# A four-layer network on one core: the second layer's block with its router's weights loaded early and another planned order

## The chip, the cores and the metric
The kernel runs on one core of one Trainium2 chip. The metric is the device time of one execution in microseconds.

## What is computed
A network of four layers on 2048 tokens of 128 features. Each layer adds an attention-like branch and an expert branch to x, both computed from the normalised x. The change touches the second layer alone:

```python
def _L1_attn_ref(x, Wq, Wk, Wv, Wf, g_norm_w, Wo):
    q = _swish((x @ Wq).reshape(b, t, H, K))
    k = _swish((x @ Wk).reshape(b, t, H, K))
    v = (x @ Wv).reshape(b, t, H, V)
    f = jax.nn.log_sigmoid((x @ Wf).reshape(b, t, H, M)) / GATE_LOGIT_NORMALIZER
    s = 1.0 - jnp.exp(f)
    o = _gsa_recurrence(q, k, v, s, f, scale=K ** (-0.5))
    o = o * jax.lax.rsqrt(jnp.mean(o * o, axis=-1, keepdims=True) + NORM_EPS) * g_norm_w
    return o.reshape(b, t, H * V) @ Wo

def _L1_ffn_ref(tokens, gate_w, W1, b1, W2, b2):
    probs = jax.nn.softmax(x @ gate_w.T, axis=-1)
    top2_w, top2_idx = jax.lax.top_k(probs, 2)
    counts = jnp.bincount(top2_idx.reshape(-1), length=E)
    keep = (counts <= cap).astype(x.dtype)
    comb = jnp.zeros((T, E), dtype=x.dtype).at[jnp.arange(T)[:, None], top2_idx].add(top2_w)
    comb = comb * keep[None, :]
    h = jax.nn.relu(jnp.einsum('th,ehf->tef', x, W1) + b1[None, :, :])
    y = jnp.einsum('teh,ehf->tef', h, W2) + b2[None, :, :]
    out = jnp.einsum('te,tef->tf', comb, y)
```

The recurrence keeps, per head, a state that is decayed by gates at every token; the kernel computes it in chunks of 64 tokens.

## The kernel before
Features lie on the 128 partitions, tokens along them. The tokens are two halves of 1024, and all is f32. The function `layer_1_branches` holds the whole second layer's block: the attention branch for both halves and the expert branch (eight experts, four quarters of 512 tokens, 32 steps j) run interleaved on TensorE, ScalarE and VectorE.

The attention branch, for each half: `projections` multiply the tokens with the weights `wt` (keys, values, gates by token; L1536), four pairs of products, each pair copied from PSUM by ScalarE (L1737). `log_of_sigmoid` forms the gates on ScalarE (absolute value L1744, exponential L1748, logarithm L1752), VectorE ends them in `gates` (L1879). `sums_of_gates` (L1554, L1556) and `gates_at_ends` (L1568, 16 products with 4 columns) sum them over tokens; `queries_or_keys` are products with `wq` through `product` (L108), `added` (L1586) makes what every chunk adds to the state, `states` (L1905) chains the 14 chunks on VectorE in 28 operations, which end with the scaling at L1911, and `states_turned` (L1597) turns them by 64 small products. Then come eight tiles of 128 tokens for each half: keys by queries (L1611, L1616), the mask on VectorE (L1922), logits (L1626), a softmax over VectorE and ScalarE (L1935 to L1954), transposes (L1635, L1638), their copy by ScalarE (L1831), slots by slots (L1649), a mask (L1962), outputs (L1659, L1664). At the end the mean of squares, the norm and the product with `wo`.

The expert branch: the router's product (`routing.logits`, L1007) and its choices on VectorE, an exponential on ScalarE (L1030), the counts (L1018), the turn to rows (L1024) and a store of the routing weights `comb` to memory (L995). From there SyncE loads a row of `comb` spread over all partitions for each step (`l_cs`, L1494) and a small piece for the bias product (`l_comb`, L1484). Step j: the first product (L108, tile `l_w1s`), relu on ScalarE (L1864), the weighing on VectorE (L1990), the second product summed in PSUM (L1716). Each quarter's sum starts with the bias product (L1713) and is added to x by VectorE (L1997). Three buffers hold the hidden values and the spread rows.

The order on each engine is written by a plan: every operation is a generator step that yields a planned time, and `in_order` sorts an engine's steps by these times (`PLAN_HALF` by half, `PLAN_TILE` by tile, `PLAN_EXPERT` by step). The same times set which of three PSUM slots a result takes, and so what it must wait for:

```python
def in_order(*programs):
    ahead = [[next(p, None), p] for p in programs]
    while any(time is not None for time, p in ahead):
        first = min((n for n, (time, p) in enumerate(ahead) if time is not None), key=lambda n: ahead[n][0])
        ahead[first][0] = next(ahead[first][1], None)
```

Only the order of the times matters, not their values. Semaphores carry all dependences, so a step waits if its inputs are late. Blocks of different layers are separated by a barrier of all engines.

Of the kernel before, what the change touches and what calls it, by code (L numbers as in the profile page):

```python
# [12 lines left out]
D = 128  # L13
# [33 lines left out]
class Core:  # L47
# [27 lines left out]
    def sem(self, name):  # L75
        self.taken.append(self.nc.alloc_semaphore(name))
        return self.taken[-1]
# [1154 lines left out]
def layer_0_output(core, cols, x1):  # L1232
# [4 lines left out]
    with ExitStack() as ctx:  # L1237
# [41 lines left out]
    "raw": ((-1081.249, -1077.137, -1042.271, -1024.881), (-1011.753, -941.228, -773.834, -752.792)),  # L1279
    "copy_raw": ((-1075.619, -1037.111, -970.597, -922.579), (-711.412, -622.755, -601.399, -519.594)),  # L1280
    "q": ((-475.959,), (451.442,)),
    "q_silu": ((-172.152,), (588.372,)),
    "k": ((-326.269,), (583.701,)),
    "kt_silu": ((-126.114,), (703.013,)),
    "abs": ((-878.111,), (-516.284,)),
    "exp": ((-725.621,), (-409.285,)),
    "ln": ((-674.441,), (-217.181,)),
    "f": ((-925.510,), (-654.044,)),
    "expf": ((-588.789,), (43.256,)),
    "s": ((-887.741,), (-81.622,)),  # L1290
    "D": ((-714.095, -640.152, -317.000, -294.344), (-249.299, 133.889, 490.244, 533.240)),
    "decays": ((-556.237, -351.939, -94.621, -14.229), (-66.260, 511.555, 656.344, 668.213)),
    "eg": ((-381.908, -343.173, -118.829, 45.012), (55.472, 548.470, 686.294, 691.310)),
    "weights": ((-692.871, -671.130, -211.073, -102.260), (-74.956, 121.898, 490.122, 561.874)),
    "ends": ((-644.216,), (-219.247,)),
    "decay_ends": ((-272.821,), (125.503,)),
    "add": ((-129.287, -108.606), (665.011, 676.767)),
    "copy_add": ((421.957, 453.205), (764.074, 794.772)),
    "states": ((-57.796, -18.779, 171.653, 263.587), (652.682, 702.699, 710.536, 745.507)),
    "scale": ((334.169,), (750.775,)),  # L1300
    "Skt": ((625.370,), (1350.808,)),
    "copy_Skt": ((709.734,), (1295.597,)),
    "square": ((1352.872,), (1411.883,)),
    "mean": ((1421.698,), (1491.541,)),
    "log": ((2544.424,), (3617.117,)),
    "rstd": ((3341.839,), (4064.410,)),
    "scaled": ((3612.555,), (4066.440,)),
    "out": ((4071.457,), (5267.780,)),
    "join": ((4089.228,), (4246.270,)),
    "k_silu": ((-180.112,), (171.365,)),  # L1310
}
PLAN_TILE = {
    "A": (704.440, 1365.757),
    "mask_A": (651.820, 1450.125),
    "L": (710.156, 1370.819),
    "lg": (658.341, 1456.286),
    "soft": (805.839, 1338.538),
    "norm": (659.343, 1459.812),
    "T": (717.401, 1378.542),
    "copy_T": (809.914, 1344.911),  # L1320
    "B": (718.082, 1380.008),
    "mask_B": (665.065, 1464.168),
    "O": (723.357, 1384.516),
    "copy_O": (814.259, 1350.264),
}
PLAN_EXPERT = {
    "hidden": (-986.666, -848.766, -723.734, -624.912, -407.809, -325.502, -258.983, -133.205, -80.466, 302.035, 474.836, 531.890, 625.094, 661.711,
        711.318, 718.337, 738.819, 766.229, 822.014, 1225.173, 1360.244, 1373.418, 1381.800, 1402.399, 1418.613, 1428.896, 2604.976, 3173.687,
        3563.369, 4059.409, 4177.355, 4298.075),
    "relu": (-732.131, -624.941, -552.867, -304.909, -180.719, -129.717, -79.314, 141.992, 193.548, 521.253, 624.829, 697.552, 707.962, 735.468,  # L1330
        806.695, 819.352, 840.576, 857.238, 1214.835, 1291.321, 1318.674, 1345.054, 1356.302, 1379.255, 1393.381, 2575.189, 3350.433, 3501.179,
        3565.950, 4065.778, 4246.291, 4292.431),
    "weigh": (-752.536, -727.210, -694.226, -656.618, -471.742, -408.385, -249.266, -96.387, 40.067, 61.793, 125.045, 550.246, 562.989, 646.471,
        677.977, 687.350, 695.614, 790.153, 1362.310, 1409.461, 1449.578, 1467.566, 2536.958, 3282.350, 3320.613, 3469.474, 3567.542, 3583.767,
        4070.138, 4114.201, 4123.695, 4124.013),
    "add": (-595.909, -377.501, -333.886, -226.051, -190.628, -166.810, 3.203, 37.949, 580.705, 598.643, 629.913, 705.892, 712.623, 716.751, 752.963,
        755.712, 824.914, 1364.972, 1366.185, 1372.704, 1388.344, 1416.763, 1446.606, 1448.758, 3170.214, 3404.566, 3591.788, 3989.248, 4250.325,
        4302.464, 5146.025, 5160.432),
    "cs": (-919.034, -843.901, -830.537, -394.140, -306.056, -305.801, -204.452, -109.561, 349.895, 351.828, 373.491, 454.101, 607.007, 687.599,
        690.334, 750.696, 750.930, 1361.245, 1368.714, 1420.148, 1496.241, 2548.207, 2548.946, 3158.556, 3355.408, 3360.017, 3427.646, 3595.730,  # L1340
        4140.388, 4174.676, 4182.187, 4307.648),
    "b2": (-638.253, 509.912, 810.290, 2570.119),
    "join": (20.309, 715.071, 3462.675, 4126.088),
# [1824 lines left out]
```

## Time and profile before

| | us |
|---|---|
| three runs | 1866.88, 1859.01, 1863.92 |
| median | 1863.92 |
| the profiled execution | 1868.61 |
| its span | 1866.9 |
| mean granted TensorE clock | 0.949 |
| TensorE busy over the span | 1695.0 (91%) |
| VectorE busy | 1310.5 (70%) |
| ScalarE busy | 1229.2 (66%) |

The span is what the profiler's instructions cover; the execution's own time is 1.7 us longer. Names in the profile have no number (`l_raw` is `l1_raw0` or `l1_raw1`); PE is TensorE, PEld its weight loads, DVE VectorE, ACT ScalarE, SP SyncE, whose queue issues the loads. A product of 512 columns in f32 shows as two records, so that "x2" stands for one of them.

### The profile page before, as it was taken

The page shows a single profiled execution, that of the slowest core. Times are in us where ns is not written, and L with a number is a line of the kernel's source. Part 1 is how long each engine was busy: PE and PEld are TensorE (multiplying, and loading weights), DVE is VectorE, ACT ScalarE, POOL GpSimd, SP SyncE. Part 2 cuts the span into 40 slices and gives each one's busy share as a digit, 9 for nine tenths or more (in the row PEclk, how much of TensorE's full clock was granted, in tenths as well). Part 3 has the DMA queues.
Part 4 walks back from the last instruction along what each step waited for, and adds up shares of the span by engine and source line. Part 5 has one row for each costly group of instructions (what it writes and reads, how often), then busy time and mean ns, then how long its engine had stood idle before and what let it go on. Part 6 is the DMA issues. An engine that isn't in the chain of part 4 may idle for free. (4 is left out here: it accounts for less than half of the span.)

```text
span 1866.9 us, 19526 instructions
## 1 busy us (share of the span) xinstructions
PE 1695.0 (91%) x6936; PEld 700.4 (38%) x6944; DVE 1310.5 (70%) x1793; ACT 1229.2 (66%) x1541; POOL 109.2 (6%) x159
## 2 busy tenths in 40 slices
PE   4599999999999999996899599997898989997998
PEld 2133333333333333322443356563243333333665
DVE  4677777777777777741333237773999999996897
ACT  2488888888888888883132287334786767772663
POOL 1000111111111111011000100000000000000000
PEclk8799999999999999998799699998899999999999
DMA  3400000000001000000131121111344444541000
GB/s 102 131 6 12 23 12 23 12 24 12 24 12 24 12 7 12 1 1 2 59 113 56 33 54 47 42 29 28 110 139 158 146 158 141 171 162 34 6 1 23
DMA packets 48136, 100.76 MB, mean 54 GB/s; under 512 B 7719, under 2 KB 21126, under 8 KB 46740
## 3 DMA queue, kind: packets, MB, share of 16 engines
q1 hardware_dynamic: 48042, 99.54, 17.2%
q8 instruction: 55, 0.90, 0.2%
q14 instruction: 39, 0.32, 0.1%
HBM read 91.55 MB, written 7.87 MB: 53 GB/s over the span
## 5 line engine op out<-in xcount | busy, mean ns | idle before, releaser
L727 DVE TENSOR_REDUCE best<-quad 128x2 f32<-128x1024 f32 x256 | 309.6, 1221 | 130.5 <-PE quad L517 128.0
L641 ACT ACTIVATE weights<-quad 128x1024 f32<-128x1024 f32 x256 | 255.4, 1027 | 28.9 <-PE quad L542 28.6
L108 PE MATMUL quad<-xn,l_w1s 128*128 128x512 f32 x288 | 151.1, 632 | 9.8 <-DMA l_w2s<-in_F_w 7.6
L2400 ACT ACTIVATE l_hid<-quad,l_w1s 128x512 f32<-128x512 f32 x112 | 75.2, 686 | 99.5 <-PE quad L108 98.9
L559 PE MATMUL quad<-weights,values 128*32 128x512 f32 x1024 | 136.4, 605 | 0.4 <-ACT weights L641 0.4
L2262 PE MATMUL quad<-l_st,ident 128*128 128x512 f32 x256 | 121.3, 602 | 5.8 <-DVE l_st L2466 5.7
L108 PE MATMUL quad<-q,wf 128*128 128x512 f32 x256 | 121.5, 606 | 0.7 <-DVE mk L698 0.3
L2308 PE MATMUL quad<-l_hid,l_w2s 128*128 128x512 f32 x224 | 105.7, 601 | 15.5 <-DVE l_hid L2497 15.5
L108 PE MATMUL quad<-hid,wf 128*128 128x512 f32 x256 | 116.6, 599 | 0.0
L585 ACT ACTIVATE hid<-quad,col 128x512 f32<-128x512 f32 x128 | 84.7, 686 | 21.7 <-PE quad L108 21.5
L517 PE MATMUL quad<-ks,qs 48*128 48x512 bf16 x512 | 89.5, 385 | 7.0 <-DVE best L727 6.4
L542 PE MATMUL quad<-qs,ks 49*128 49x512 bf16 x512 | 91.5, 384 | 2.2 <-ACT weights L641 2.2
L1213 ACT ACTIVATE e_hid<-quad,e_w1s 128x1024 f32<-128x1024 f32 x32 | 35.6, 1113 | 83.7 <-PE quad L108 83.7
L108 PE MATMUL quad<-sq_all,mean_w 128*128 128x512 f32 x176 | 89.6, 621 | 0.2 <-POOL sq_all L753 0.2
L108 PE MATMUL quad<-cur,wa 128*128 128x512 f32 x168 | 87.1, 627 | 0.0
L1229 DVE TENSOR_TENSOR e_hid<-e_hid,e_cs 128x1024 f32<-128x1024 f32 x32 | 38.5, 1222 | 67.5 <-ACT e_hid L1213 48.0
L108 PEld LDWEIGHTS quad<-xn,l_w1s 128*128 128x128 f32 x288 | 53.0, 196 | 86.3 <-issue 54.1
L2449 DVE TENSOR_TENSOR l_st<-l_u,l_bs 128x1024 f32<-128x1024 f32 x64 | 76.0, 1213 | 3.2 <-PE quad L2262 3.2
L753 POOL TENSOR_TENSOR sq_all<-cen_all 128x512 f32<-128x512 f32 x64 | 65.2, 1039 | 217.2 <-DVE cen_all L672 217.2
L542 PEld LDWEIGHTS quad<-qs,ks 49*128 49x128 bf16 x512 | 22.2, 93 | 146.8 <-issue 60.4
L2466 DVE TENSOR_TENSOR l_st<-l_st,l_c_rows 128x1024 f32<-128x1024 f32 x64 | 75.9, 1214 | 0.0
L2262 PEld LDWEIGHTS quad<-l_st,ident 128*128 128x128 f32 x256 | 49.2, 194 | 70.3 <-issue 59.4
(379 smaller groups left out, 3064.4 us busy)
## 6 DMA issues: line engine op xcount, KB each, us to landing
l_bs<-xd_dram SPq DMA_DIRECT2D x32, 512.0 KB, 4.8
l_c_rows<-xd_dram SPq DMA_DIRECT2D x32, 512.0 KB, 4.6
l_cs<-comb SPq DMA_DIRECT2D x28, 512.0 KB, 4.8
e_cs<-comb SPq DMA_DIRECT2D x8, 1024.0 KB, 5.2
l_cs<-comb SPq DMA_DIRECT2D x32, 256.0 KB, 3.3
wf<-in_L_f SPq DMA_DIRECT2D x16, 256.0 KB, 2.6
l_w1s<-in_F_w SPq DMA_DIRECT2D x28, 129.0 KB, 2.1
l_w2s<-in_F_w SPq DMA_DIRECT2D x28, 128.0 KB, 2.3
```

The lines of the kernel that those rows point to most:

```text
L108: last = nc.tensor.matmul(out[:, c:c + BANK], lhsT, rhs[:, c:c + BANK], start=(n == 0), stop=(n == len(pairs) - 1))
L517: last = nc.tensor.matmul(to[:, par * BANK:(par + 1) * BANK], qs[n % BUFS][rows, slot, qt * P:(qt + 1) * P], ks[n % BUFS][rows, slot, c * ...
L542: last = nc.tensor.matmul(to[:, par * BANK:(par + 1) * BANK], ks[n % BUFS][rows, slot, kt * P:(kt + 1) * P], qs[n % BUFS][rows, slot, c * ...
L559: last = nc.tensor.matmul(out[32 * j:32 * j + 32, :], values[:, kt, GH * g + j, :], weights[p % BUFS][:, j % 2, j // 2, :], start=(kt == 0 ...
L585: return nc.scalar.activation(*args, ACT.Gelu_apprx_tanh, **kwargs)
L641: nc.scalar.activation(weights[p % BUFS][:, slot, :, :].rearrange("p a t -> p (a t)"), doubles.of("weigh", m, i), ACT.Exp, scale=scale).th ...
L727: nc.vector.tensor_reduce(heads[:, :, slot, qt, c], doubles.of("search", m, i).rearrange("p (a t) -> p a t", a=2), AX.X, ALU.max).then_inc ...
L2262: last = nc.tensor.matmul(y[d][:, c:c + BANK], core.ident[:, :], st[n % RING][:, c:c + BANK], start=False, stop=(s == NS - 1), skip_group_ ...
L2308: last = nc.tensor.matmul(total[c], w2s[p][:, f, :], hid[j % HIDS][:, f, :], start=False, stop=False, skip_group_check=True)
L2400: nc.scalar.activation(hid[j % HIDS][:, f, :], ring.of("hidden", j, f), ACT.Gelu, bias=w1s[p][:, F + f:F + f + 1]).then_inc(hidden_read, 1)
L2449: nc.vector.tensor_tensor(st[n % RING][:, :], u[h][d][:, :], bs[k % 2][:, :], ALU.mult).then_inc(dbx_ready, 1)
L2466: nc.vector.tensor_tensor(st[n % RING][:, :], st[n % RING][:, :], cs_rows[k % 2][:, :], ALU.mult).then_inc(times_c, 1)
```

## The change
Three edits. The router's weights are loaded second instead of eighth. The load of the query and key weights `wq` counts on a semaphore of its own, on which each of the four products with `wq` waits; the start of TensorE's program waits for `wt` alone. And all planned times of the block are new, of which two lines of 62 stand here:

```diff
 PLAN_HALF = {
-    "raw": ((-1081.249, -1077.137, -1042.271, -1024.881), (-1011.753, -941.228, -773.834, -752.792)),
+    "raw": ((-1580.895, -1575.614, -415.628, -352.666), (-1568.371, -350.926, -286.483, -159.875)),
...
-    landed, wo_landed, built = sem("landed"), sem("wo_landed"), sem("built")
+    landed, wq_landed, wo_landed, built = sem("landed"), sem("wq_landed"), sem("wo_landed"), sem("built")
...
                 sp.dma_start(wt[:, :], a["A1_tok"]).then_inc(landed, 16)
-                sp.dma_start(wq[:, :], a["A1_qk"]).then_inc(landed, 16)
+                routing.load(sp)
+                sp.dma_start(wq[:, :], a["A1_qk"]).then_inc(wq_landed, 16)
                 sp.dma_start(wo[:, :], a["A1_wo"]).then_inc(wo_landed, 16)
                 for h in range(GH4):
                     sp.dma_start(gain[GK * h:GK * h + GK, :], a["A1_gain"]).then_inc(wo_landed, 16)
-                routing.load(sp)
...
                 def queries_or_keys(h, name, ready):
                     u = "qk".index(name)
                     yield pre(name, h)
+                    pe.wait_ge(wq_landed, 16)
                     ring_free(pe, name, h, 0)
...
-                pe.wait_ge(landed, 32)
+                pe.wait_ge(landed, 16)
```

From the edit at `wq_landed` on, lines of the changed kernel are one higher. What the new times move is shown at three places. The first is ScalarE's start of the block: copies of the tokens' products (L1737, now L1738), the absolute value, the routing's exponential. Before:

```order
L1737 ACTIVATE l1_raw0<-quad0 128x1024 x2
L1737 ACTIVATE l1_raw0<-quad1 128x1024
L1737 ACTIVATE l1_raw0<-quad0 128x1024
L1744 ACTIVATE l1_se0<-l1_raw0 128x2048
L1730 ACT_TABLE_LOAD
L1030 ACTIVATE l1_route_exps<-l1_route_exps 128x128
L1864 ACTIVATE l1_hid0<-quad1,l1_w1s 128x512
```

And now:

```order
L1738 ACTIVATE l1_raw0<-quad0 128x1024 x2
L1738 ACTIVATE l1_raw1<-quad1 128x1024
L1738 ACTIVATE l1_raw0<-quad0 128x1024
L1731 ACT_TABLE_LOAD
L1030 ACTIVATE l1_route_exps<-l1_route_exps 128x128
L1738 ACTIVATE l1_raw0<-quad0 128x1024
L1745 ACTIVATE l1_se0<-l1_raw0 128x2048
L1865 ACTIVATE l1_hid0<-quad1,l1_w1s 128x512
```

The routing's exponential has moved ahead of the absolute value and of the first half's last copy; the third copy is of the second half. The second place is VectorE behind the routing: weighings of hidden values, the gates (L1879, now L1880). Before:

```order
L1098 COPY l1_route_turned_comb<-quad1 128x128
L1879 SCALAR_TENSOR_TENSOR l1_raw0<-l1_raw0,l1_se0 128x8x256
L1883 TENSOR_SCALAR l1_add0<-l1_add0 128x2048
L1990 TENSOR_TENSOR l1_hid0<-l1_hid0,l1_cs0 128x512
L1990 TENSOR_TENSOR l1_hid1<-l1_hid1,l1_cs1 128x512
```

And now:

```order
L1098 COPY l1_route_turned_comb<-quad1 128x128
L1991 TENSOR_TENSOR l1_hid0<-l1_hid0,l1_cs0 128x512
L1991 TENSOR_TENSOR l1_hid1<-l1_hid1,l1_cs1 128x512
L1880 SCALAR_TENSOR_TENSOR l1_raw0<-l1_raw0,l1_se0 128x8x256
L1991 TENSOR_TENSOR l1_hid2<-l1_hid2,l1_cs2 128x512
```

Two weighings, each with its spread row from memory, now stand ahead of the first half's gates. The third place is TensorE at the end of the first half's last two tiles (transposes L1638, slots L1649, outputs L1659 and L1664; each one higher now). Before:

```order
L1638 MATMUL quad0<-ident,l1_lg2 128x128 x2
L1649 MATMUL quad0<-l1_turned2 128x128 x4
L1659 MATMUL quad0<-l1_Am2,l1_raw0 32x128 x4
L1664 MATMUL quad0<-l1_turned2,l1_add0 32x64 x8
L1635 MATMUL quad0<-ident,l1_se0 128x128 x2
L1638 MATMUL quad0<-ident,l1_lg3 128x128 x2
L1649 MATMUL quad0<-l1_turned3 128x128 x4
L108 MATMUL quad1<-xn,l1_w1s 128x512
L1659 MATMUL quad0<-l1_Am3,l1_raw0 32x128 x4
```

And now:

```order
L1639 MATMUL quad0<-ident,l1_lg2 128x128 x2
L1717 MATMUL quad1<-l1_hid0,l1_w2s 128x512
L1650 MATMUL quad0<-l1_turned2 128x128 x4
L1598 MATMUL quad1<-l1_zeros,l1_add1 32x64 x4
L1598 MATMUL quad1<-ident,l1_add1 32x64 x60
L1660 MATMUL quad0<-l1_Am2,l1_raw0 32x128 x4
L1665 MATMUL quad0<-l1_turned2,l1_add0 32x64 x8
L1636 MATMUL quad0<-ident,l1_se0 128x128 x2
L1639 MATMUL quad0<-ident,l1_lg3 128x128 x2
L1717 MATMUL quad1<-l1_hid1,l1_w2s 128x512
L1650 MATMUL quad0<-l1_turned3 128x128 x4
L108 MATMUL quad1<-xn,l1_w1s 128x512
```

Two expert sums and the turning of the second half's states, which came after the tiles, stand between them now. In the second half's tiles, in turn, five tiles in a row have no expert product between them; before there was one in most.

## Rows read from the trace of the kernel before

**Rows 1.** Windows: length, busy us of PE, PEld, DVE, ACT, POOL; PEclk, DMA, GB/s
```profile
1059.00:1275.00 216.00, 202.53 (x1819) 122.81 (x1819) 130.89 (x303) 109.11 (x154) 4.92 (x31) 0.92 0.19 48
1099.00:1104.00 5.00, 5.00 (x7) 1.76 (x7) 1.29 (x2) 3.47 (x5) 0.00 (x0) 0.50 0.58 90
1145.00:1190.00 45.00, 44.25 (x661) 29.89 (x660) 37.79 (x92) 21.32 (x35) 0.00 (x0) 1.00 0.14 39
1194.00:1200.00 6.00, 5.31 (x42) 2.61 (x38) 5.02 (x18) 1.15 (x3) 0.00 (x0) 0.50 0.00 0
```

**Rows 2.** Timeline, block's start: start us, us, engine, line, operation, count [idle before <-releaser]
```profile
1059.34 0.34 SPq L1464 DMA_DIRECT2D l_wt<-in_A_tok  x1
...
1059.72 0.43 SPq L1465 DMA_DIRECT2D l_wq<-in_A_qk  x1
...
1062.54 0.42 SPq L987 DMA_DIRECT2D l_route_w<-in_F_router  x1
...
1064.29 5.90 PE L1007 MATMUL quad<-l_route_w,xn 128*128 128x8 f32 x27 [9.70 <-DMA l_route_w<-in_F_router]
```

**Rows 3.** DMA issues of 1059 to 1064 us: KB each, us to landing
```profile
l_wt<-in_A_tok SPq DMA_DIRECT2D x1, 256.0 KB, 2.7
```

**Rows 4.** DMA issues of 1290 to 1300 us, the third layer's start
```profile
l_route_w<-in_F_router SPq DMA_DIRECT2D x1, 7.0 KB, 4.3
```

**Rows 5.** Timeline, the routing's exponential and what waits for it
```profile
1080.93 1.91 ACT L1744 ACTIVATE l_se<-l_raw 128x2048 f32<-128x2048 f32 x1
...
1085.93 0.39 PE L1018 MATMUL quad<-l_route_load,mean_w 128*128 128x8 f32 x2 [1.80 <-DVE l_route_load L1084]
...
1092.07 0.67 PE L1554 MATMUL quad<-l_raw,l_rel 128*128 128x256 f32 x2 [0.38 <-ACT l_raw L1737]
```

**Rows 6.** Timeline, the store of the routing weights, spread rows and gates
```profile
1087.75 0.60 SPq L995 DMA_DIRECT2D comb<-l_route_turned_comb  x1
1089.88 1.28 SPq L1494 DMA_DIRECT2D l_cs<-comb  x3
...
1089.67 2.29 DVE L1879 SCALAR_TENSOR_TENSOR l_raw<-l_raw,l_se 128x2048 f32<-128x2048 f32 x1 [1.95 <-ACT l_se L1752]
```

**Rows 7.** Tile l_cs, all 32 loads of the block
```profile
DMA to landing us min/median/max: 3.0/3.3/6.0
```

**Rows 8.** Timeline of TensorE, end of the first half's tiles; last row from the end
```profile
1192.06 0.71 PE L1649 MATMUL quad<-l_turned 64*128 64x128 f32 x8 [0.69 <-ACT l_turned L1831]
1193.63 0.50 PE L1659 MATMUL quad<-l_Am,l_raw 128*32 128x128 f32 x8 [0.86 <-DVE l_Am L1962]
...
1196.46 1.22 PE L1649 MATMUL quad<-l_turned 64*128 64x128 f32 x8 [0.69 <-ACT l_turned L1831]
1197.61 2.07 PE L108 MATMUL quad<-xn,l_w1s 128*128 128x512 f32 x2
...
1201.81 1.12 PE L108 MATMUL quad<-xn,l_w1s 128*128 128x512 f32 x2
1202.77 1.02 PE L1716 MATMUL quad<-l_hid,l_w2s 128*128 128x512 f32 x2
...
1254.40 1.88 PE L108 MATMUL quad<-sq_all,l_heads 128*128 128x512 f32 x4
```

**Rows 9.** Timeline of TensorE, the second half's tiles
```profile
1209.20 0.71 PE L1611 MATMUL quad<-sq_all,l_kt 64*128 64x128 f32 x8 [0.53 <-ACT l_send L1817]
...
1226.04 0.71 PE L1611 MATMUL quad<-sq_all,l_kt 64*128 64x128 f32 x8
...
1230.50 0.71 PE L1611 MATMUL quad<-sq_all,l_kt 64*128 64x128 f32 x8
...
1235.37 0.72 PE L1611 MATMUL quad<-sq_all,l_kt 64*128 64x128 f32 x8
...
1250.16 0.72 PE L1649 MATMUL quad<-l_turned 64*128 64x128 f32 x8 [0.69 <-ACT l_turned L1831]
```

**Rows 10.** Timeline of VectorE, the scaling that ends a half's states
```profile
1200.02 2.23 DVE L1911 TENSOR_TENSOR l_add<-l_add,l_ends 128x960 f32<-128x960 f32 x2
```

More of the change, by code:

```diff
@@ L1288 @@
[L1288 to L1305, printed above, removed]
@@ new lines @@
+    "weights": ((-50.321, 755.376, 843.753, 848.533), (1514.057, 1525.649, 1680.677, 1729.672)),
+    "ends": ((231.854,), (986.181,)),
+    "decay_ends": ((857.885,), (1098.550,)),
+    "add": ((1574.525, 1584.281), (2102.023, 2112.373)),
+    "copy_add": ((2505.899, 2549.893), (2985.709, 2989.305)),
+    "states": ((1696.355, 1980.000, 2644.887, 2656.230), (2726.647, 2942.474, 2945.464, 2970.313)),
+    "scale": ((2681.014,), (3037.400,)),
+    "Skt": ((2526.495,), (2979.793,)),
+    "copy_Skt": ((3119.875,), (3217.354,)),
@@ L1311 @@
+    "square": ((3238.834,), (13549.288,)),
+    "mean": ((3190.301,), (13506.655,)),
+    "log": ((13419.396,), (13923.299,)),
+    "rstd": ((13889.254,), (13969.301,)),
+    "scaled": ((13416.150,), (13533.290,)),
+    "out": ((13900.092,), (14096.747,)),
+    "join": ((13563.678,), (14097.220,)),
+    "k_silu": ((1190.511,), (1120.572,)),
 }
 PLAN_TILE = {
[L1313 to L1324, printed above, removed]
+    "A": (2923.687, 3134.954),
+    "mask_A": (3031.933, 3219.629),
+    "L": (2929.289, 3140.564),
+    "lg": (3038.201, 3225.124),
+    "soft": (3166.696, 3350.062),
+    "norm": (3042.363, 3226.683),
+    "T": (2936.194, 3147.984),
+    "copy_T": (3170.468, 3352.244),
@@ L1342 @@
[L1342 to L1351 removed]
+    "hidden": (-298.163, -253.668, -140.919, -84.812, 780.855, 919.924, 939.445, 1030.080, 1122.956, 1151.335, 1284.201, 1574.042, 1808.544,
+        2048.518, 2112.350, 2141.572, 2517.344, 2674.724, 2926.783, 2933.188, 2966.161, 2971.943, 2986.234, 3143.206, 3188.193, 3196.659, 3389.005,
+        13236.423, 13483.791, 13510.350, 13563.602, 13886.754),
@@ L1352 @@
+    "b2": (-134.838, 1346.631, 2926.430, 3217.086),
+    "join": (926.530, 2947.016, 3302.077, 13603.221),
+    "comb": (-134.535, 896.909, 1575.183, 2054.189),
+    "route": (-350.152, -317.194, -315.724, -271.617),
+    "logits": (-1699.373,),
+    "count": (-307.419,),
+    "turn": (-294.816,),
+    "choice": (-283.017,),
+    "store": (-314.758,),
+    "stored": (-244.448,),
 }
```

66 lines of the change are left out of this document (30 added, 36 removed).

## The prediction
> **What bounds the kernel now.** I read the engines' busy time over the block first. The second layer's block runs from the issue of its first load at 1059.34 us [rows 2] to about 1275 us. TensorE is busy 202.5 of the 216 us there, VectorE 130.9 and ScalarE 109.1 [rows 1]. So TensorE's work sets the length, and an order of instructions can win only two things: time in which TensorE waits, and time in which it works at the lower of its two clock levels (a granted clock of 0.50, which is 1.2 of 2.4 GHz). The other layers are not touched and are separated from this one by barriers.
>
> Then I read the timeline for TensorE's waits. The largest are: 9.70 us before the first router product, of which 4.95 lie after 1059.34 (the rest belongs to the norm before) [rows 2]; 1.80 us before the product for the counts [rows 5]; three waits of 0.69 to 0.86 us where the first half's last tiles end [rows 8]; 0.53 us for the second half's first tile and 0.69 us at its last [rows 9]. Low clock shows from 1099 to 1104 us, although TensorE was then busy all the time, and from 1194 to 1200 us, behind the first two of the three waits [rows 1, 8].
>
> **The change, part by part.** All terms are against the profiled execution; minus is shorter.
>
> *Start.* TensorE begins when the first tokens' weights and the router's weights have landed. Before, the router's load is the eighth issued, at 1062.54, and the first product starts at 1064.29, 1.75 us after that [rows 2]. Now it is second, issued at 1059.72 where the query and key weights were, and the start no longer waits for those. The tokens' weights land 2.7 us after 1059.34, at 1062.04 [rows 3]. For the router's load standing behind a 256 KB load I have two bounds: those 1.75 us, where it stood behind small loads, and 4.3 us in the third layer, where it is third behind 256 KB [rows 4]. I take 2.7, as the load just ahead of it took: it lands at 1062.4, and **-1.85 us** is won, with bounds -2.2 (the tokens' weights are then the later) and -0.2. The added wait for the query and key weights costs nothing: their first product comes behind the gates' first products, which start at 1092 [rows 5]. On SyncE the router's load passes six others, which are issued one place later; none is wanted before the first expert's weights, which keep their place. Nothing is moved on GpSimd.
>
> *Counts.* ScalarE's exponentials for the routing stood behind the absolute value of 2048 columns, 1.91 us [rows 5]; now they come before it. The product for the counts can start 1.85 + 1.91 earlier, at 1082.17. TensorE has one product of 512 columns fewer ahead of it (0.86 us at full clock: two take 1.88 and one 1.02 with its end [rows 8]) and is free at 1085.93 - 1.80 - 1.85 - 0.86 = 1081.4. The wait shrinks from 1.80 to 0.76: **-1.04**.
>
> *Two new waits right behind.* The bias product of the experts used to come late, behind the gates' products; now it comes behind the counts, the turn (0.35 us for both), three expert products and four of the tokens: 7 x 0.86 + 0.35 later, at 1088.55. The store of the routing weights followed the counts by 1.82 us and the first load from it by 2.13 [rows 6]; so that load is issued at 1086.12, the small one for the bias product at 1086.55, and at 3.0 us to landing, the quickest of the large loads [rows 7], it is there at 1089.55: **+1.0** (bounds 0, if it lands as fast as a store, and +4.0 at the 6.0 us of the slowest load of such rows [rows 7]). Behind it VectorE weighs the first two experts before it forms the gates of the first half (2.29 us, [rows 6]), and the second of these waits for a 256 KB load. Three such loads end 6.0 us after the third's issue, so I put the second's at 4.5 us, 1091.5. The gates are then done at 1091.5 + 0.69 + 2.29 = 1094.5; TensorE wants them at 1093.0 after four more products. That is 1.5 us where 0.38 stood [rows 5]: **+1.1** (0 to +3).
>
> *Entry into the tiles.* The second half's chain of states, 28 small operations that stood among the tiles, now lies nearly whole ahead of the first mask, and the scaling that ends it, 2.23 us on VectorE [rows 10], stands between the first tile's mask and its logits. It is ready about when TensorE's logits are, so it is in the way; TensorE has the next tile's products (about 1.0 us) and an expert product to cover it, and what follows needs the second mask, which is late too, by an estimated 0.4: 2.23 + 0.4 - 1.0 - 0.86 = **+0.8** (0 to +3).
>
> *End of the first half.* There TensorE had nothing of its own to do between a transpose and its copy. Now two expert sums, one expert product and the 64 small products that turn the second half's states stand in exactly these places. The three waits go: 0.69 + 0.86 + 0.69 = **-2.24**. With them should go the low clock behind them: the small products took 1.22 instead of 0.71 us, the expert product 2.07 instead of 1.12, and I estimate 0.2 us for each of the four groups of small products beside them [rows 8]: **-2.3**. The bound is half the 5.3 us busy at that level, -2.65, and 0 if the clock stays low.
>
> *Turned states ready early*, so the second half's first tile need not wait for their copy: **-0.53** [rows 9].
>
> *Tiles without a filler.* In the steady stretch VectorE sets the pace when TensorE has no expert work: 4.46 us for a tile, against 4.87 with a product that takes 0.96 us start to start [rows 8, 9]. A tile without filler thus loses 4.46 - (4.87 - 0.96) = 0.55 us. There were five such tiles, there are eight now, five of them in a row: **+1.65**.
>
> *Tail.* An expert sum fills the 0.69 us before the last tile: **-0.69**. The 21 products behind it find their inputs at the pace of the old ones; the chain of the last norm ends while they run.
>
> Sum: -1.85 - 1.04 + 1.0 + 1.1 + 0.8 - 2.24 - 2.3 - 0.53 + 1.65 - 0.69 = **-4.1 us**. The profiled execution took 1868.6, the median of the three runs is 1863.9; against the median that gives **1859.8 us**. The largest term is the low clock behind the waits, and it is the least sure one. The rows show a fall behind a stretch with waits of at most 0.86 us, and another at 1099 us with TensorE busy throughout [rows 1, 8]. The Trainium skill (TensorE: Matmul & The Clock Gate, "What's actually happening") says that the clock falls after TensorE has been idle for long enough; waits this short would then not have caused the fall, and filling them would not lift it. By that rule the sum would be -1.8.
>
> **The rivals.**
> - *The low clock stays or only moves* (20%). For it: the fall at 1099 shows that full busy time does not protect, and the filler there is partly small products. Against it: from 1145 to 1190 us, where such small products and whole tiles ran, the clock stayed up [rows 1]. Then -2.3 is missing: 1862.1 us.
> - *The early start doesn't happen* (7%). The router's load takes 4.3 us as in the third layer; TensorE starts at 1064.1. Then 1.65 of the 1.85 is missing: 1861.5 us. For it, the only row of a router load close behind a large one; against it, that one had another small load between, and was not waited for alone.
> - *More low clock goes* (20%). The falls in the block's first third (1099 to 1104) follow the tiny products for the gates at the ends, whose surroundings change. If one of them goes too, half of 5 us is won, 2.5, and with the two new waits at their lower bounds 2.1 more: -8.7, or 1855.2 us. If a second of these falls goes, 2.5 more: 1852.7.
> - *Slower: new falls of the clock* (10%). The waits ahead of the gates put idle time right before the tiny products, and five tiles in a row without filler leave TensorE 12% idle. If the clock falls once in each place, each at half of 5.3 us (2.65), and the new waits come out in the middle of their upper halves (+2.5), the result is -4.1 + 5.3 + 2.5 = +3.7: 1867.6 us. It decides as soon as both falls are there. Against it: of the tiles between 1165 and 1190 us three were unfilled, and the clock stayed at 1 [rows 1].
>
> **How the numbers follow.** The forecast itself gets 43%, with 1857 to 1863 as its own range. About 0.5%, 9.3 us, is what a measurement of this kernel can tell from no change. All cases but the best end of the third lie inside it, and the slower rival too; so "same" gets most: faster 0.16 (most of the third rival's lower part, and a spread of the runs of some 4 us either way), slower 0.03, same 0.81. The range 1853.5 to 1866 takes in the first three rivals and half of the slower one.
>
> **What would show it.** In the profile of the changed kernel the first router product should start near 1062.4 us, the counts' near 1082.2, with waits of about 1 us ahead of the bias product and 1.5 us ahead of the gates' products. The first half's last tiles should show no wait over 0.3 us and a granted clock of 1. The block's last sum should end near 1271. A first product at 1064, a low clock between the halves, or a new low stretch in the second half's tiles would each point to its rival. A wait of TensorE over 2 us in the stretch from 1110 to 1160, where I expect none, would show the whole reading wrong.

## The result and the profile after

The changed kernel takes 1861.5 us (median of 20 runs, 1858.1 to 1866.2) against 1867.8 us for the kernel before (20 runs on the same chips, 1858.9 to 1877.5). The ratio is 0.9967, with a 95% interval of 0.9955 to 0.9979: 6.2 us, or 0.33%, faster. The profiled execution took 1860.27 us.

Two executions differ by some microseconds outside the change too: the block's first load is issued at 1059.34 us before and at 1060.86 now, with the same program ahead of it. So I measure the block itself, from the issue of its first load to the end of the last sum into x: 1274.92 - 1059.34 = **215.58 us** before and 1270.23 - 1060.86 = **209.37 us** now, 6.21 less. Over the block TensorE is idle 13.07 us before and 8.97 now; the other 2.11 us are busy time. The work is the same, so busy time differs mainly by the clock at which it is done.

The same windows as [rows 1], of the changed kernel (length, busy us of PE, PEld, DVE, ACT, POOL; PEclk, DMA share, GB/s):

```profile
1061.00:1276.00 215.00, 204.66 (x1829) 124.25 (x1830) 130.52 (x302) 110.35 (x155) 4.79 (x31) 0.94 0.19 48
1100.00:1105.00 5.00, 5.00 (x14) 3.67 (x15) 0.34 (x1) 4.93 (x3) 0.00 (x0) 0.50 0.28 67
1145.00:1190.00 45.00, 44.18 (x589) 27.31 (x588) 41.10 (x114) 22.69 (x33) 0.00 (x0) 1.00 0.17 49
1194.00:1200.00 6.00, 6.00 (x68) 3.91 (x66) 4.65 (x12) 2.61 (x7) 0.00 (x0) 1.00 0.01 3
```

The last row was 5.31 us busy at 0.50 before [rows 1]: the low clock between the halves is gone. The one at 1100 is still there. The block's start and the routing, against [rows 2, 3, 5, 6], from the timeline of the changed kernel, with one row of its DMA issues at the end:

```profile
1060.86 0.34 SPq L1464 DMA_DIRECT2D l_wt<-in_A_tok  x1
...
1061.24 0.42 SPq L987 DMA_DIRECT2D l_route_w<-in_F_router  x1
...
1063.86 6.97 PE L1007 MATMUL quad<-l_route_w,xn 128*128 128x8 f32 x32 [7.75 <-DMA l_route_w<-in_F_router]
...
1084.53 0.39 PE L1018 MATMUL quad<-l_route_load,mean_w 128*128 128x8 f32 x2 [0.72 <-DVE l_route_load L1084]
...
1091.41 1.09 PE L1714 MATMUL quad<-l_comb,l_b2s 8*128 8x512 f32 x2 [0.27 <-issue]
...
1094.13 0.69 DVE L1991 TENSOR_TENSOR l_hid<-l_hid,l_cs 128x512 f32<-128x512 f32 x1 [1.39 <-DMA l_cs<-comb]
1094.74 2.28 DVE L1880 SCALAR_TENSOR_TENSOR l_raw<-l_raw,l_se 128x2048 f32<-128x2048 f32 x1
...
1094.87 1.13 PE L1717 MATMUL quad<-l_hid,l_w2s 128*128 128x512 f32 x2 [0.46 <-DVE l_hid L1991]
...
1097.12 1.03 PE L1569 MATMUL quad<-l_at_ends,l_raw 128*128 128x4 f32 x8 [1.12 <-issue]
```

```profile
l_route_w<-in_F_router SPq DMA_DIRECT2D x1, 4.0 KB, 2.5
```

TensorE's first product starts at 1063.86, 3.00 us after the first issue, where it was 4.95. The counts wait 0.72 instead of 1.80; their product comes 23.67 us after the first issue, where it was 26.59. The second weighing waits for its row of routing weights, and VectorE forms the gates only behind it; TensorE pays 0.46 and 1.12 us for that. These are the new waits that the prediction put at 1.5 us. At the end of the first half [rows 8] TensorE now goes through without a wait:

```profile
1199.13 1.02 PE L1717 MATMUL quad<-l_hid,l_w2s 128*128 128x512 f32 x2
1200.09 0.72 PE L1650 MATMUL quad<-l_turned 64*128 64x128 f32 x8
...
1200.87 1.85 PE L1598 MATMUL quad<-ident,l_add 64*32 64x64 f32 x120
1202.66 0.42 PE L1660 MATMUL quad<-l_Am,l_raw 128*32 128x128 f32 x8
```

**The low clock.** In the first 15 us behind the first issue every version has a granted clock of 0.50 (1.2 of 2.4 GHz). Behind them the kernel before has three stretches at a granted clock of 0.50, the changed one two, and the second is shorter. Windows of exactly these stretches, before and after:

```profile
1098.24:1105.10 6.86, 6.86 (x12) 2.94 (x11) 1.67 (x3) 4.20 (x6) 0.00 (x0) 0.50 0.52 85
1122.18:1128.98 6.80, 6.80 (x28) 3.23 (x31) 1.29 (x2) 3.11 (x5) 0.00 (x0) 0.50 0.11 36
1193.90:1200.70 6.80, 6.11 (x62) 3.02 (x54) 5.76 (x19) 1.56 (x3) 0.00 (x0) 0.50 0.00 0
```

```profile
1099.80:1106.60 6.80, 6.80 (x20) 5.14 (x20) 1.79 (x2) 5.56 (x4) 0.00 (x0) 0.50 0.22 53
1120.30:1123.70 3.40, 3.40 (x9) 2.19 (x9) 0.18 (x1) 3.33 (x6) 0.00 (x0) 0.50 0.33 79
```

So 20.5 us of low clock have become 10.2. In this pair of profiles the norm behind the block gained as well, 3.1 us that the block's length doesn't hold: its eight products on x take 3.67 us instead of 6.75. These are the first product rows behind the block, of the trace before and of the trace after:

```profile
1276.39 6.75 PE L108 MATMUL quad<-x,centre_w 128*128 128x512 f32 x8 [2.73 <-PEq L86]
```

```profile
1271.73 3.67 PE L108 MATMUL quad<-x,centre_w 128*128 128x512 f32 x8 [2.75 <-PEq L86]
```

### The profile page after: what moved, and what is told of

Read it like the earlier page. It is cut to its first block and busy times, and to the rows that moved or that the text cites. A ratio compares the mean times of both kernels' runs of the same rounds, so it can differ in the third digit from the quotient of the medians.

```text
span 1858.5 us, 19528 instructions
## 1 busy us (share of the span) xinstructions
PE 1689.4 (91%) x6936; PEld 700.0 (38%) x6944; DVE 1310.6 (71%) x1793; ACT 1227.5 (66%) x1539; POOL 109.1 (6%) x159
```

## The experiments

Each kernel ran in five rounds beside the kernel before. Since single executions differ by several us, three numbers of each kernel's one profile stand beside the ratio: the block's length as defined above, TensorE's idle time in it, and the time at a clock of 0.50 in it, after the first 15 us (from windows of 2 us, so good to 0.1). A profile is a single execution: a load that lands a microsecond later in it is in these numbers too.

| kernel | ratio to before (95%) | block us | TensorE idle | low clock |
|---|---|---|---|---|
| before | 1 | 215.58 | 13.07 | 20.4 |
| changed | 0.9967 (0.9955 to 0.9979) | 209.37 | 8.97 | 10.3 |
| 1 loads alone | 0.9950 (0.9937 to 0.9964) | 209.39 | 11.50 | 6.8 |
| 2 order alone | 0.9971 (0.9957 to 0.9985) | 212.04 | 11.01 | 13.7 |
| 3 no fillers at the half's end | 0.9999 (0.9987 to 1.0011) | 215.04 | 12.41 | 13.6 |
| 4 gates first | 0.9958 (0.9942 to 0.9974) | 208.19 | 8.03 | 10.2 |
| 5 filled tiles | 0.9960 (0.9946 to 0.9975) | 208.63 | 8.10 | 13.6 |
| 6 small products spread | 0.9977 (0.9968 to 0.9987) | 211.38 | 9.07 | 13.6 |
| 7 = 4 + 5 + 6 | 0.9907 (0.9892 to 0.9922) | 200.82 | 6.97 | 0 |
| 8 loads, fillers on the old order | 1.0006 (0.9997 to 1.0016) | 218.57 | 17.29 | 20.4 |
| 9 = 4 + 6 | 0.9933 (0.9912 to 0.9954) | 203.73 | 8.36 | 0 |
| 10 = 7 without fillers | 0.9944 (0.9924 to 0.9964) | 205.66 | 11.26 | 0 |
| 11 = 7, old loads | 0.9928 (0.9907 to 0.9949) | 204.69 | 10.48 | 3.4 |
| 12 loads, spread, on the old order | 0.9999 (0.9985 to 1.0012) | 215.85 | 13.47 | 17.0 |

Block less idle is TensorE's busy time: 193.9 to 195.4 us where there is no low clock (7, 9, 10), 200.4 with 10.3 us of it (changed), 202.5 with 20.4 (before). The work is the same. So two columns, idle and low clock, explain most of the third, though not all of it: a straight line through the fourteen busy times leaves up to 2.4 us (kernel 3 is busy 202.6 us with 13.6 us of low clock, kernel 8 only 201.3 with 20.4).

### The two parts apart

Loads alone: the plan's tables of the kernel before, with the loads of the changed one. Order alone is the opposite:

```diff
+                routing.load(sp)
+                sp.dma_start(wq[:, :], a["A1_qk"]).then_inc(wq_landed, 16)
-                sp.dma_start(wq[:, :], a["A1_qk"]).then_inc(landed, 16)
...
-                routing.load(sp)
```

> The kernel before with the new order of the loads and the separate wait for the first two weights alone; every engine keeps the old order of work. Theory A (terms of the sum stand apart): TensorE starts about 3.0 us after the block's first load is issued, against 4.95 in the kernel before, so about 1.9 us come off there; the waits of the gates' product (0.38), of the counts (1.80) and at the end of the first half stay or grow by what the engines that TensorE waits for do not start earlier. Ratio to the kernel before about 0.999, block about 213.7 us against 215.6. Rival B (the early start is only worth anything with the new order, because the weighings, the router's load and VectorE come no earlier): start earlier by 1.9 but the counts wait grows to 2.5 or more, block within 0.7 us of 215.6. Rival C (the low clock decides): a start that is 1.9 us earlier lets the clock stay low for longer or fall at another place; then the block is over 1 us off in either direction and the windows of the granted clock show where.

> The changed kernel with the old order of the loads (both weights of the first products ahead of the router's, one shared wait) and the new order of work on all engines. Theory A (terms stand apart): TensorE starts about 4.9 us after the block's first load again, everything behind it as in the changed kernel: block 209.4 + 1.9 = 211.3 us, ratio to the kernel before about 0.998. The short waits at the bias product (0.27), the weighings and the gates (0.46 and 1.12) shrink if they come from VectorE and a DMA being late against TensorE. Rival B (the new order needs the early load): the waits at the counts and the gates do not shrink and the block is at 212 or more. Rival C (the clock): low-clock stretches move with the start; end of first half stays at full clock (no stretch below 0.9 between 135 and 145 us after the block's start) since no wait is there.

Measured: 209.39 us with the loads alone, as short as with the whole change, and 212.04 with the order alone. The parts give 6.2 and 3.5 us, and together 6.2: they don't add, and the loads alone are at least as good as the whole change (by the ratios too, whose intervals overlap). With the loads alone TensorE starts at 2.99 us and the counts still wait 1.79, as theory A has it. But an earlier start isn't won in full. The counts' product in that kernel:

```profile
1086.83 0.39 PE L1018 MATMUL quad<-l_route_load,mean_w 128*128 128x8 f32 x2 [1.79 <-DVE l_route_load L1084]
```

That is 25.61 us after the first issue (1061.22), against 26.59 before [rows 5] with the same wait: 0.98 us earlier, half of the 1.96 by which TensorE starts earlier. The granted clock rises at 15.0 us in both, so what is started earlier is done at 0.50. The remaining 5.2 us of the 6.2 are rival C's: the clock didn't fall at 1099 at all. The windows of that kernel (the old place of the first fall, then its two low stretches):

```profile
1097.00:1107.00 10.00, 10.00 (x37) 5.64 (x37) 5.37 (x8) 9.20 (x11) 0.00 (x0) 1.00 0.48 104
1120.60:1124.00 3.40, 3.40 (x5) 1.35 (x4) 0.49 (x1) 1.99 (x4) 0.00 (x0) 0.51 0.06 20
1192.30:1195.70 3.40, 3.40 (x18) 1.50 (x18) 2.88 (x10) 0.27 (x1) 0.00 (x0) 0.51 0.00 0
```

Its order on TensorE is that of the kernel before; there the 32 products with 4 columns began 34.5 us after the first issue, here 33.6. One microsecond went with a low stretch of 6.8 us, in one profile of each. With the order alone the start is late again (5.03 us; the counts' product 1.02 us later), and the second low stretch is 6.8 us long instead of 3.4; both together are what the loads are worth there, 2.67 us. By its number, 212.04, that is rival B, and the waits at the counts (0.72) and the gates (1.12) didn't shrink, as it has them; but the amount beyond the later start is low clock.

### The fillers at the end of the first half

```diff
-    "Skt": ((2526.495,), (2979.793,)),
+    "Skt": ((2526.495,), (2989.0,)),
-    "add": (... 2976.359, 2984.206, ...
+    "add": (... 2986.0, 2989.1, ...
-    "hidden": (... 2986.234, ...
+    "hidden": (... 2989.3, ...
```

The times of the relu and of the copy that belong to them are moved with them.

> The changed kernel with the fillers at the end of the first half taken out: the add for the second half's first tile, its hidden product, the shared expert's product and one more add go behind the second half's first big product, as in the order before. Theory A (waits and clock both come back): waits of about 0.7, 0.9 and 0.7 us on TensorE, 2.2 together, and the granted clock falls to 0.50 for 5 to 7 us there as in the kernel before, which costs 2.3 more: block 209.4 + 4.5 = 213.9, ratio to the kernel before about 0.999. Rival B (the fall of the clock was not caused by these waits but by where the low stretches earlier in the block ended): only the waits come back, clock 1.00 throughout, block 211.6. Rival C (the waits turn up elsewhere, as in tiles that go unfilled at the moment): block within 0.7 of 209.4.

The same edit once more on the best kernel, which has no low clock to confuse it:

> The kernel with all three edits (block 200.8, full clock from 15 us on) with the fillers at the end of the first half taken out again. Theory A (the waits alone): waits of 0.69, 0.86, 0.31, 0.69 and about 0.5 us come back, block 203.9, clock 1.00 there. Rival B (the waits at that place bring the clock down, as in the kernel before, where it fell 135 us from the block's start): a low stretch of 3.4 to 6.8 us between 125 and 145 and block 205.5 to 208. Ratio to the kernel before 0.992 by A, 0.993 to 0.994 by B.

Measured: without the fillers the block is 5.67 us longer in the changed kernel and 4.84 in the best one. The waits come back, with 0.31 and 0.53 us in the first kernel that its expectation had not counted. TensorE in the second of these kernels:

```profile
1196.28 0.71 PE L1644 MATMUL quad<-l_turned 64*128 64x128 f32 x8 [0.69 <-ACT l_turned L1826]
1197.86 0.43 PE L1654 MATMUL quad<-l_Am,l_raw 128*32 128x128 f32 x8 [0.86 <-DVE l_Am L1957]
...
1199.31 0.44 PE L1633 MATMUL quad<-ident,l_lg 128*128 128x128 f32 x2 [0.30 <-DVE l_lg L1949]
1200.43 0.72 PE L1644 MATMUL quad<-l_turned 64*128 64x128 f32 x8 [0.69 <-ACT l_turned L1826]
1201.08 1.13 PE L1711 MATMUL quad<-l_hid,l_w2s 128*128 128x512 f32 x2
...
1207.24 0.71 PE L1606 MATMUL quad<-sq_all,l_kt 64*128 64x128 f32 x8 [0.62 <-ACT l_send L1812]
```

That is 3.16 us. Windows of the same places in the first and in the second kernel:

```profile
1200.70:1212.70 12.00, 8.94 (x208) 5.29 (x208) 4.04 (x11) 5.21 (x10) 0.00 (x0) 1.00 0.16 23
```

```profile
1195.50:1207.50 12.00, 8.85 (x207) 5.35 (x208) 3.88 (x10) 5.36 (x10) 0.00 (x0) 1.00 0.10 23
```

TensorE idles over 3 of 12 us there and the clock stays at 1.00, in both. By the clock that is rival B in the first kernel and theory A in the second; by the length, 215.04 and 205.66 us, both blocks are longer than these have them (the second lies in its rival B's range), for the reasons below. The waits alone don't bring the clock down. In the four profiles with the old order (before, 1, 8, 12) it did fall at the end of the first half. Whether the place of the waits in time or the products around them make that difference wasn't told apart.

Most of the rest of the 4.84 is a store: TensorE waits 1.74 us for the bias product's load instead of 0.24, since the store of the routing weights took longer to land, 3.5 us against 2.1; the wait at the next weighing is 0.35 shorter for it, and busy time is 0.55 longer. These are its rows in kernels 10 and 7; in kernel 11 it took 4.0 and TensorE waited 2.26:

```profile
comb<-l_route_turned_comb SPq DMA_DIRECT2D x1, 64.0 KB, 3.5
```

```profile
comb<-l_route_turned_comb SPq DMA_DIRECT2D x1, 64.0 KB, 2.1
```

The edit doesn't touch that store; the kernel before had 2.1 too. In the changed kernel (3 against it) the idle time is 3.44 us more: 3.08 are these waits, and a weighing comes 0.57 us later. With 3.4 us more of low clock behind the second row of small products, busy time is 2.2 us more.

### Gates ahead of the weighings

```diff
-    "f": ((-163.74,), (-128.912,)),
+    "f": ((-268.0,), (-128.912,)),
```

> The changed kernel with one move on VectorE: the gates of the first half are computed ahead of the two weighings that wait for the load of the choices' positions. Theory A (TensorE's 1.12 us wait at the gates' product is VectorE's queue behind that DMA): the wait goes, the 0.46 us wait ahead of it stays or grows by what the weighings come later (the gates take 2.28 us on VectorE), net 0.5 to 1.2 us off the block. Rival B (the waits are the DMA's own time): the wait moves to the weighings' readers and the block stays at 209.4 within 0.5. Rival C: with the waits gone TensorE stays busier and the low-clock stretch from 1100 is shorter or goes, up to 3 us off.

(The load that the two weighings wait for brings rows of routing weights.) Measured: 208.19, 1.18 less; theory A. The 1.12 us wait is gone, 0.46 became 0.57:

```profile
1091.91 2.29 DVE L1870 SCALAR_TENSOR_TENSOR l_raw<-l_raw,l_se 128x2048 f32<-128x2048 f32 x1 [4.89 <-ACT l_se L1743]
1094.12 1.28 DVE L1981 TENSOR_TENSOR l_hid<-l_hid,l_cs 128x512 f32<-128x512 f32 x2
```

VectorE had been idle while it waited for the load; now the gates lie in that time. The low clock is as long as before, in other places (39 to 42 and 56 to 63 us from the first issue).

### Products in the unfilled tiles, and small products spread

Filled tiles: three first expert products, three sums, the last quarter's bias product and what belongs to them are drawn forward into the second half's tiles, so that each of five empty ones gets a product; the tail behind the last tile gets shorter by six. Spread: the 32 products with 4 columns of each half are cut in four.

```diff
-    "hidden": (... 3188.193, 3196.659, 3389.005, 13236.423, 13483.791, ...
+    "hidden": (... 3151.0, 3164.2, 3177.4, 3188.193, 3196.659, ...
...
+ENDS_AT = ((231.854, 755.3, 800.0, 853.0), (935.0, 939.5, 986.181, 1031.0))
...
-                    yield pre("ends", h)
+                    yield ENDS_AT[h][0]
...
                         for t in range(GT):
+                            if t % 4 == 0 and j + t:
+                                yield ENDS_AT[h][(j * GT + t) // 4]
```

> The changed kernel with five of the second half's tiles, which go through without an expert's product at the moment, given one each, so that the tail behind the last tile is five or six products shorter. Theory A (an unfilled tile's wait of 0.24 to 0.34 us on the masked scores, and its period of 4.46 to 4.56 us, is a gap that a product fills in part): the five waits of 0.24 to 0.34 go (1.3 us in all) and the filled tiles take less than a product more: block 209.4 less about 2, ratio to the kernel before about 0.9955. Rival B (a tile with a product costs the full 0.86 us of the product more, TensorE being full apart from the wait): only the waits go, 1.3 us. Rival C (ScalarE or VectorE sets the pace of the tiles, and the product's Relu or weighing makes them later): block at 209.4 or above.

> The changed kernel with the 32 products of 4 columns of each half (the gates' ends, 4.53 us of TensorE in the first half) cut into four groups of eight, which lie between large products. Theory A (the clock falls at 39 and at 59 us from the block's start because TensorE does little array work in those stretches, though its busy share is 3.9 and 5.0 of 5 us): at least one of the two falls goes, which gives 1.7 to 3.4 us each; block 205 to 208. Rival B (the clock falls from waits alone, and those ahead of 39 us are unchanged): both falls stay where they are, block within 0.7 us of 209.4. Rival C (the small products cost more among large ones than in a row): block above 209.4 by the extra issue time.

> The changed kernel with three edits together: gates ahead of the weighings (alone it gave a block of 208.2 against 209.4), the five filled tiles of the second half, and the products of 4 columns spread. Theory A (terms add): 209.4 less 1.2 less 2 less up to 3.4, block 203 to 206.5, ratio to the kernel before about 0.994. Rival B (the low clock moves when the work ahead of it moves, so that terms of the waits add but the clock gives some back): block 206 to 208.5 and the low stretches lie at other places than in the three alone.

> The changed kernel with two edits: gates ahead of the weighings (alone: block 208.2, low clock from 39 to 42 and from 56 to 63 us) and the products of 4 columns spread (alone: block 211.4, low clock from 39 to 42 and from 56 to 66). Theory A (both together are what keeps the clock up: without the 1.12 us wait and without a row of small products no stretch is poor enough in work): no low clock after the first 15 us, block 200.8 (all three edits) plus the 2.0 to 2.4 of the five unfilled tiles, 202.8 to 203.2. Rival B (it was the filled tiles, or chance in one run): a low stretch at 39 or 56 remains, block 205 or more.

Filling alone gave 0.74 us, because the second low stretch was 3.4 us longer in that profile; with the clock at 1.00 in both, 7 against 9, it gives 2.91, of which 1.39 are idle time. Spreading alone made the block 2.0 us longer. There is still a fall at 39 us (3.4 us long) and another, now at 56 us and 10.2 long, so theory A fails for it. Rival B's 0.7 us are passed too, and rival C has its number but not its cause: idle time is 0.1 more, and most of the rest is low clock, 3.3 us more. But gates first and spreading together leave no low clock at all, as theory A of the last expectation has it. The windows of kernels 9 and 7:

```profile
1077.00:1260.00 183.00, 178.90 (x1773) 108.08 (x1772) 122.60 (x285) 106.46 (x151) 0.00 (x0) 1.00 0.20 48
```

```profile
1075.00:1255.00 180.00, 177.24 (x1772) 108.36 (x1771) 122.36 (x285) 105.45 (x151) 0.00 (x0) 1.00 0.19 49
```

Alone, each of the two edits changed the block by -1.2 and +2.0 us; together by -5.6. Kernel 7, with the filled tiles, is the best: 1851.9 us (1851.0 to 1854.6), ratio 0.9907, by the ratios 0.6% less than the changed kernel, and below what its own theory A gave. It computes the same; only the order differs.

### The loads on the best kernel, and two edits on the old order

Kernel 11 is 7 with the old loads; 8 and 12 build on 1. In 8 the product that turns the states goes between the last transposes, and one sum a tile later:

```diff
-    "Skt": ((625.37,), (1350.808,)),
+    "Skt": ((625.37,), (765.0,)),
-    "add": (... 755.712, 824.914, ...
+    "add": (... 763.0, 1300.0, ...
-    "b2": (-638.253, 509.912, 810.29, 2570.119),
+    "b2": (-638.253, 509.912, 823.0, 2570.119),
```

> The kernel with all three edits and the old order of the loads with the shared wait. Theory A (the loads are worth their earlier start and no more, as long as the clock is the same): block 200.8 + 1.9 = 202.7, ratio to the kernel before 0.9917. Rival B (a start at another time puts the stretches of little work at another place against the clock, which falls): block 204.5 or more with a low stretch after 15 us. Rival C (the early start was partly given back in waits for the count and for VectorE): block at 201.5 to 202.

> The kernel before with the new order of the loads (alone: block 209.4, as the whole change) and, beside it, only the fillers at the end of the first half: one add ahead of the turn of the last weights but one, the product that turns the states behind it, and the products behind the last tile in another order. Theory A (what the loads gave and what the fillers give add): waits there were 0.69, 0.87, 0.31, 0.69 us, 2.56 together; two or three of them go, 1.2 to 2.0 us, and the low clock of 3.4 us in that stretch goes too, 1.0 to 1.7: block 206 to 207.5, ratio to the kernel before about 0.994. Rival B (the clock falls elsewhere instead): block 208 to 211 though the waits are gone. Rival C (the shift of the products only moves the wait to their next readers): block at 209.4 with waits of the same sum.

> The kernel before with the new order of the loads (alone: block 209.4, low clock at 59 to 63 us right behind a row of 32 products of 4 columns, and at 131 to 134 us) and those products of both halves spread in groups of eight. Theory A (the row of small products is what the fall at 59 us comes from): that low stretch goes, about 1.7 us, block 207.7, and the one at 131 stays or moves with the waits there. Rival B (the fall has to do with the time or the load and not with that row): low clock at 59 to 63 stays, block within 0.7 of 209.4. Rival C (everything behind it comes earlier and the waits at the end of the first half then bring a longer low stretch): block above 208.5 with over 3.4 us of low clock between 125 and 145.

Kernel 11: 204.69, 3.87 more than 7. By the number this is rival B, and a low stretch of 3.4 us is there, from 35.5 to 38.9 us after the first issue. But 3.51 of the 3.87 are idle time: the start is 2.14 us later, as theory A has it, and the slower store of that execution adds 1.4. Busy time is only 0.35 longer: the low stretch costs it more than that, and the later start, of which the counts' product sees 1.07 us, gives about as much back.

Kernel 8 has a longer block than the kernel before, by none of the three theories. The filler wasn't ready; TensorE, and then VectorE's operation that it waited for:

```profile
1192.53 1.22 PE L1640 MATMUL quad<-l_turned 64*128 64x128 f32 x8 [0.69 <-ACT l_turned L1822]
1198.38 0.44 PE L1588 MATMUL quad<-l_zeros,l_add 64*32 64x64 f32 x8 [4.62 <-DVE l_add L1902]
```

```profile
1196.09 2.23 DVE L1902 TENSOR_TENSOR l_add<-l_add,l_ends 128x960 f32<-128x960 f32 x2
```

In the old order VectorE chains the states among the tiles and scales them behind the last one (second fence), so TensorE stood still for 4.62 us, at a clock of 0.50. The changed order also brings the chain ahead of the tiles; there the last scaling ends at 1167.1 and the turn starts at 1200.9.

Kernel 12: the fall at 59 us is gone, as theory A says, but the block is 6.5 us longer than in 1; by number and by place of the low clock at the end it is rival C. In the old order the row of small products covered ScalarE's next copy; cut in four, only a quarter stands there:

```profile
1093.04 0.95 PE L1563 MATMUL quad<-l_at_ends,l_raw 128*128 128x4 f32 x8
1095.96 0.67 PE L1547 MATMUL quad<-l_raw,l_rel 128*128 128x256 f32 x2 [1.97 <-ACT l_raw L1732]
```

The clock then fell at 42 us instead, for 6.8 us, and for 10.2 us at the end of the first half.

## Why the prediction was right, and where not

The forecast was 1859.8 us, 4.1 below the median shown and 8.8 below the profiled execution. Measured were 1861.5 and, for the kernel before, 1867.8: the three runs shown had given a median 3.9 us under that of 20, and the change gave 2.1 more than the sum. The two errors partly cancel, and that the forecast came within 1.7 us is luck to that extent. By term, with the block as the measure:

| term | predicted | measured |
|---|---|---|
| start | -1.85 | -1.95 at the first product, -0.98 at the counts |
| counts | -1.04 | -1.08 |
| bias product, weighing, gates | +1.0 + 1.1 | 0.27 + 0.46 + 1.12 - 0.38 = +1.47 |
| entry into the tiles | +0.8 | 0 (one wait of 0.17 us, as before) |
| waits at the end of the first half | -2.24 | -2.24 |
| low clock behind them | -2.3 | gone (6.8 us of it, 6.11 of them busy) |
| turned states ready early | -0.53 | -0.53 |
| three more unfilled tiles | +1.65 | 2.91 / 5 x 3 = +1.75 (from 7 against 9) |
| wait ahead of the last tile | -0.69 | -0.69 |
| second low stretch 3.4 us shorter | not in the sum | up to -1.7 |

With -0.98 for the start, the terms other than low clock add up to -2.30. The block gave -6.21, so 3.9 us are left for the 10.3 us of low clock that went, where the sum had 2.3.

- The waits were read rightly, one by one. The largest miss is low clock, 1.6 us more than forecast: of three low stretches the prediction lists two, and the one from 1122.18 us, of which half went, isn't among them.
- The second is the start. Its load landed as forecast, but half of what it wins is given back, since the clock stays at 0.50 until 15.0 us in both kernels and the work started earlier is done there. The prediction counted the 1.85 in full at the counts' and at the bias product too; these come 0.8 and 1.1 us later than it has them, by their offsets from the first issue.
- The third is the entry into the tiles. I let the scaling of the states on VectorE reach TensorE, and no new wait shows there.
- The bias product waited 0.27 and not 1.0: between the store's issue and the first load lie 2.14 us, as predicted, but the small load was read by TensorE 2.56 us after its issue, where I had taken 3.0, and TensorE came 1.1 us later than computed.
- *End of the first half*: the amount came out, the reason given for it doesn't hold. "With them should go the low clock behind them" made the low clock a consequence of the three waits. Put back into the changed order in experiments 3 and 10, the waits left the clock at 1.00. What does bring the clock down there in the old order stays open.
- The third rival, more low clock goes, is what happened in part: the sum held nothing for the falls in the block's first third, and one of them was halved.
- *The early load* by itself is worth about 1 us, and what came with it differs: 6.2 us on the old order and 2.7 on the new one, where the surplus is low clock that goes; 3.9 on kernel 7, where it is the slower store of one execution and a low stretch.
- The slower rival, new falls of the clock in the gap ahead of the gates, has such a place, the 1.12 us wait with the row of small products behind it. But a fall was there in the kernel before already, also 38.9 us after the first issue and without that wait, so nothing new was lost. Taking the wait or the row away alone (4, 6) left 3.4 us of this fall; taking both, in 9, removed it.
- The rule weighed there (the Trainium skill, TensorE: Matmul & The Clock Gate, "What's actually happening": a fall follows enough idle time) gave -1.8. This case's traces bear out one half of it: waits of at most 0.86 us, over 3 of 12 us in all, brought no fall in experiments 3 and 10. They disagree with it as the whole story: the second fall in the changed kernel comes with TensorE busy for 23 us without a wait, and the kernel before falls at 1122.2 us with no wait since 1092.1.

## What to carry to other kernels

When TensorE's clock can fall, the parts of a change don't add, and of an earlier start into a stretch of low clock only half was won here: first count waits, then look for stretches of low clock, and judge an edit from both columns, not from its time alone. Two edits of which one looks small and the other harmful alone (here gates first and the spread, -1.2 and +2.0 us) can be worth 5.6 together. A filler must be ready where it is put, and a row of small work that is moved may have been somebody's cover.

## What had not been expected

- **The clock fell with no wait ahead of it.** The second fall of the changed kernel, at 1120.3, stands at the end of 3.86 us of products with 4 columns, ahead of which TensorE had no wait since 1097.1:

```profile
1116.16 1.02 PE L1717 MATMUL quad<-l_hid,l_w2s 128*128 128x512 f32 x2
1117.02 3.86 PE L1569 MATMUL quad<-l_at_ends,l_raw 128*128 128x4 f32 x32
1120.74 2.05 PE L108 MATMUL quad<-xn,l_w1s 128*128 128x512 f32 x2
```

That the row of small products is its cause isn't shown: in experiment 6 the row is cut up and the clock falls 3.4 us earlier still, and in experiment 1 the first such row passes without a fall. Only gates first and the spread together, in 7, 9 and 10, left no fall.

- **A fall depends on the moment as well.** The clock rises 15 us after the block's first issue in all fourteen profiles, whether TensorE starts at 2.93 or at 5.09 us; and a shift of the same order by 1 us, in experiment 1, removed a fall. The Trainium skill says in the section named above that what watches TensorE doesn't start anew with the kernel, so that a change of the clock depends on where the work lands; the shift agrees with that. But the moments themselves did not shift between executions: the rise comes at 15.0 us in all fourteen, and falls come again and again at the same offsets from the first issue (38.9 us in seven profiles, 59.4 in six), within 0.1 us, though the issue itself lies anywhere from 1058.5 to 1061.7 us. What an edit changed was the work that met them.
- **What low clock costs.** Kernel 4 has 10.2 us of it and kernel 9, nearly the same work, none: 208.19 - 203.73 = 4.46 us, and 9 idles 0.33 us more. Busy time differs by 4.79, which is 0.47 us for each microsecond of low clock. Other pairs give about the same: 0.49 for 5 against 7, and 0.41 for the kernel before against 1, once 0.98 us are added for the start.
- **The same store landed after 2.1 us in some executions and after 3.5 and 4.0 in others**, and a product that stands right behind its load waited 1.5 and 2.0 us longer for it; part of that came back at the next wait.
